# A decoder layer on one core: the hand-written timetable of its engines with many of its places changed

## What is computed

```python
# x, ctx: (4, 512, 512) f32; 16 heads of 32; I = 2048
kqv = x @ Wqkv + bqkv                       # q, k, v
scores = einsum('bsnh,btnh->bnst', k, q) / sqrt(32)
scores = triu(scores) + -10000 * tril(ones, k=-1)
out = einsum('bnkq,bknh->bqnh', softmax(scores, axis=2), v) @ Wo + bo
x = layernorm(x + out)
x = layernorm(x + wkv(w, u, k=x, v=ctx))    # a recurrence over the 512 tokens, per channel
g, up = x @ dequant(gate_w).T, x @ dequant(up_w).T
x = layernorm(x + (silu(g) * up) @ dequant(down_w).T)
```

## Time and profile before

| | us |
|---|---|
| median of 3 runs | 736.33 (734.25 to 738.01) |
| the profiled execution, its own time | 735.65 |
| its span | 733.9 |
| PE busy in the span | 679.5 (93%) |
| DVE, ACT, POOL busy | 548.9, 458.4, 380.2 |

### The profile page before, as it was taken

How to read it: one execution, slowest core, us unless ns; L and a number is a source line. 1 busy time by engine, 2 the same in 40 slices (tenths; PEclk the granted TensorE clock), 3 DMA queues, 4 the chain that set the end, 5 groups by cost and what they waited for, 6 DMA issues and landing times. The chain is left out here.

```text
span 733.9 us, 12511 instructions
## 1 busy us (share of the span) xinstructions
PE 679.5 (93%) x4290; PEld 382.2 (52%) x4290; DVE 548.9 (75%) x1268; ACT 458.4 (62%) x1096; POOL 380.2 (52%) x491
## 2 busy tenths in 40 slices
PE   8889869899996999889899999989999899999997
PEld 3335434445453455445454454534454698568855
DVE  4586735878999898899866598986898778466644
ACT  5698848978798469887764742355552565346620
POOL 6035633753989924774486645485584333303321
PEclk9998989999999999999999999998999999999999
DMA  7868653342315134453053010000000000010001
GB/s 242 248 203 218 164 127 96 117 127 69 116 51 152 35 82 131 116 118 63 2 94 87 1 58 15 29 15 0 1 1 33 25 2 1 1 57 2 1 15 44
DMA packets 45024, 54.33 MB, mean 74 GB/s; under 512 B 5921, under 2 KB 33825, under 8 KB 44961
## 3 DMA queue, kind: packets, MB, share of 16 engines
q1 hardware_dynamic: 41264, 46.85, 21.0%
q0 software_dynamic: 3264, 6.29, 5.2%
q10 hardware_dynamic: 432, 0.39, 0.2%
HBM read 45.00 MB, written 12.71 MB: 79 GB/s over the span
## 5 line engine op out<-in xcount | busy, mean ns | idle before, releaser
L1495 DVE CUSTOM_DVE_ANT_0 ee<-psb,mask,clip 128x512 f32<-128x512 f32 (+3 forms) x256 | 131.0, 537 | 30.4 <-PE psb L1025 29.0
L1263 ACT ACTIVATE ee<-ee,nm 128x512 f32<-128x512 f32 (+3 forms) x256 | 142.2, 559 | 1.9 <-DVE nm L1495 1.9
L1901 POOL TENSOR_TENSOR hl<-ring,hh 128x512 f16<-128x512 f32 x64 | 78.9, 1244 | 97.9 <-ACT hh L1382 62.9
L1273 ACT ACTIVATE ee<-psb 128x512 f32<-128x512 f32 (+1 forms) x192 | 95.6, 522 | 38.2 <-PE psb L1042 24.8
L1832 POOL TENSOR_SCALAR_AFFINE_SELECT ee<-ee 128x256 f32<-128x256 f32 x128 | 55.2, 439 | 76.2 <-ACT ee L1273 75.8
L1170 PE MATMUL psb<-wd,hl 128*128 128x512 f16 x240 | 91.0, 379 | 0.2 <-POOL hl L1901 0.2
L1168 PE MATMUL psb<-wd,hh 128*128 128x512 f16 x240 | 91.0, 379 | 0.0
L1025 PE MATMUL psb<-ks,qs 128*128 128x512 f16 (+3 forms) x256 | 74.4, 308 | 14.2 <-DMA ks<-parts 9.7
L1042 PE MATMUL psb<-qs,ks 128*128 128x256 f16 (+3 forms) x256 | 62.2, 308 | 9.4 <-ACT ee L1273 8.0
L1599 DVE RECIPROCAL ek<-ek 128x128 f32<-128x128 f32 x64 | 58.1, 932 | 6.8 <-POOL ek L1869 6.8
L982 PE MATMUL psb<-xh,wqk 128*128 128x512 f16 x240 | 60.5, 379 | 0.7 <-ACT wqk L1240 0.4
(11 more groups left out here) (213 smaller groups left out, 1630.0 us busy)
## 6 DMA issues: line engine op xcount, KB each, us to landing
qs<-parts SPq DMA_DIRECT2D x48, 128.0 KB, 2.7
ks<-parts SPq DMA_DIRECT2D x45, 128.0 KB, 2.9
parts<-qhl SPq DMA_DIRECT2D x16, 256.0 KB, 2.2
parts<-khl SPq DMA_DIRECT2D x16, 256.0 KB, 2.5
x<-in_x SPq DMA_DIRECT2D x4, 1024.0 KB, 6.6
ct<-in_ctxT SPq DMA_DIRECT2D x4, 1024.0 KB, 5.0
out<-x SPq DMA_DIRECT2D x16, 256.0 KB, 2.0
xt<-in_xT SPq DMA_DIRECT2D x14, 256.0 KB, 3.1
```

What stands on the lines that cost most here:

```text
L1263: e.activation(dst, dst, ACT.Exp, bias=NM[:, n % 4, col:col + 1], scale=-1.0, accum_out=DEN[:, n % 4, col:col + 1]).then_inc(sem("exp"), 1)
L1273: e.activation(ET[H % ET_SLOTS][:, base:base + width], PSB[:, bank["turn", H, item], 0:width], ACT.Exp, scale=SC).then_inc(sem("et"), 1)
L1495: e.tensor_tensor_reduce(E[H % E_SLOTS][:, EOFF[i]:EOFF[i] + w], PSB[:, bank["score", H, i], 0:w], MASK[:, S - w:S], -SC, CLIP[:, i:i + 1] ...
L1901: e.tensor_tensor(HS[it][1][:], pair(b, it // 2)[:, it % 2, :] if b in SEVEN else ring(b, it)[1], HS[it][0][:], ALU.subtract).then_inc(sem ...
```

## The change

Only numbers of the timetable change, and one tuple by which `oh` of groups 0 and 1 is made by ACT instead of POOL. Nothing is added or removed. `WAIT['expand']` is read by nothing. The diff is cut to its core; the rest of the moves, in SV_AT, SPREAD_AT, PV_AT, MQ_AT, MT_AT, WU_ZERO, WG_AT, BO_AT, WO_IN, WD_AT and most of TURN_AT, are of one to five slots:

```diff
-V0_AT = (3, 11)
-QK_AT = {... 3: (17, 26), ... 6: (72, 78), 7: (77, 85), 8: (103, 113), ... 11: (144, 152), ... 15: (216, 222)}
-V_AT = {1: (56, 62, 63, 72), ...}
-WO_AT = {0: (98, 103, 105, 115), ...}
+V0_AT = (0, 11)
+QK_AT = {... 3: (18, 25), ... 6: (73, 80), 7: (78, 86), 8: (103, 117), ... 11: (144, 150), ... 15: (216, 224)}
+V_AT = {1: (54, 61, 63, 74), ...}
+WO_AT = {0: (98, 101, 104, 111), ...}
-EX_AT = {... 4: 94, 5: 109, 6: 125, ... 9: 174, ...}
+EX_AT = {... 4: 86, 5: 106, 6: 121, ... 9: 169, ...}
-WIDE_AT = {... 1: 62, ... 3: 90, ... 5: 123, ... 8: 171, ...}
+WIDE_AT = {... 1: 55, ... 3: 88, ... 5: 122, ... 8: 171, ...}
-STACK_AT = {2: 18, 3: 34, 4: 51, 5: 63, 6: 82, 7: 98, 8: 114, 9: 131, 10: 148, ...}
+STACK_AT = {2: 22, 3: 30, 4: 54, 5: 62, 6: 83, 7: 98, 8: 116, 9: 131, 10: 148, ...}
-WAIT_IN = {'r1': 3, 'norm': 2, 'ek': 0, ...}
+WAIT_IN = {'r1': 0, 'norm': 2, 'ek': 1, ...}
-PIECE_AT = {'load_second': 35, ...}
-WU_AT = (41, 48, 48, 51)
+PIECE_AT = {'load_second': 31, ...}
+WU_AT = (42, 47, 49, 52)
-XLOAD = {1: (2, 2, 20, 26), ..., 3: (125, 140, 147, 162)}
-XSPLIT = {1: (13, 20, 27, 34), ..., 3: (147, 155, 159, 168)}
+XLOAD = {1: (0, 5, 21, 26), ..., 3: (126, 139, 148, 163)}
+XSPLIT = {1: (16, 21, 30, 35), ..., 3: (149, 155, 162, 165)}
-WKV_AT = {..., (3, 0): 1027, (3, 1): 1033, (3, 2): 1035, (3, 3): 1038}
-YT_AT = {..., 1: (1012, 1012, 1013, 1013), 2: (1025, 1028, 1030, 1032), 3: (1044, 1045, 1046, 1050)}
-X2_AT = {..., 2: (1036, 1036, 1036, 1036), ...}
+WKV_AT = {..., (3, 0): 1023, (3, 1): 1033, (3, 2): 1035, (3, 3): 1041}
+YT_AT = {..., 1: (1013, 1013, 1014, 1014), 2: (1026, 1030, 1031, 1032), 3: (1045, 1046, 1047, 1048)}
+X2_AT = {..., 2: (1037, 1037, 1037, 1037), ...}
-ZERO_IN = (3, 5, 5, 7, 8, 8, 9, 9, 9, 10, 11, 11, 12, 12, 12, 14)
-WS_AT = {1: (1020, 1023), 2: (1022, 1027), 3: (1017, 1023), 4: (1031, 1038)}
+ZERO_IN = (5, 7, 7, 10, 10, 10, 11, 11, 11, 12, 12, 13, 14, 14, 15, 17)
+WS_AT = {1: (1020, 1023), 2: (1025, 1027), 3: (1017, 1020), 4: (1032, 1038)}
 TURN_AT: places of turns in groups 0 to 14; of group 2
-  2: ((18, 19, 20), (23, 24, 25), (26, 28, 33), (30, 31, 33))
+  2: ((16, 17, 18), (22, 22, 23), (26, 28, 33), (24, 31, 33))
-OH_POOL = (1, 1, 1, 1, 1, 1, 0, 0, 1, 1, 1, 1, 1, 1, 0, 0)
+OH_POOL = (0, 0, 1, 1, 1, 1, 0, 0, 1, 1, 1, 1, 1, 1, 0, 0)
```

More of the change, by code:

```diff
@@ L69 @@
 W_SPLIT = (9, 14, 15, 19)
-V0_AT = (3, 11)
[L71 to L74, removed]
+V0_AT = (0, 11)
+QK_AT = {2: (12, 19), 3: (18, 25), 4: (37, 44), 5: (44, 50), 6: (73, 80), 7: (78, 86), 8: (103, 117), 9: (124,
+         132), 10: (131, 139), 11: (144, 150), 12: (169, 173), 13: (176, 199), 14: (204, 207), 15: (216, 224)}
@@ L75 @@
+V_AT = {1: (54, 61, 63, 74), 2: (116, 124, 137, 146), 3: (178, 190, 193, 203)}
+WO_AT = {0: (98, 101, 104, 111), 1: (165, 168, 174, 176), 2: (227, 231, 233, 243)}
 EARLY_AT = (246, 276)
-EX_AT = {0: 29, 1: 48, 2: 63, 3: 79, 4: 94, 5: 109, 6: 125, 7: 141, 8: 156, 9: 174, 10: 191, 11: 205, 12: 218,
-         13: 236, 14: 251, 15: 263}
-SV_AT = {0: 34, 1: 52, 2: 66, 3: 82, 4: 98, 5: 114, 6: 130, 7: 146, 8: 162, 9: 177, 10: 196, 11: 210, 12: 226,
+EX_AT = {0: 29, 1: 48, 2: 63, 3: 80, 4: 86, 5: 106, 6: 121, 7: 141, 8: 156, 9: 169, 10: 191, 11: 206, 12: 219,
+         13: 238, 14: 251, 15: 263}
@@ L80 @@
+SV_AT = {0: 34, 1: 53, 2: 66, 3: 83, 4: 98, 5: 114, 6: 130, 7: 150, 8: 162, 9: 177, 10: 198, 11: 210, 12: 226,
          13: 242, 14: 259, 15: 268}
-SPREAD_AT = {0: 34, 1: 50, 2: 66, 3: 82, 4: 98, 5: 113, 6: 128, 7: 146, 8: 161, 9: 176, 10: 194, 11: 210, 12:
-             226, 13: 243, 14: 257, 15: 268}
-PV_AT = {0: 36, 1: 54, 2: 68, 3: 86, 4: 101, 5: 117, 6: 133, 7: 151, 8: 168, 9: 184, 10: 200, 11: 214, 12: 229,
+SPREAD_AT = {0: 32, 1: 50, 2: 65, 3: 82, 4: 98, 5: 114, 6: 128, 7: 146, 8: 160, 9: 176, 10: 194, 11: 210, 12:
+             224, 13: 243, 14: 257, 15: 268}
@@ L84 @@
+PV_AT = {0: 36, 1: 54, 2: 68, 3: 87, 4: 101, 5: 117, 6: 133, 7: 151, 8: 168, 9: 184, 10: 200, 11: 214, 12: 229,
          13: 245, 14: 261, 15: 272}
-WIDE_AT = {0: 43, 1: 62, 2: 77, 3: 90, 4: 103, 5: 123, 6: 139, 7: 152, 8: 171, 9: 185, 10: 203, 11: 219, 12: 235,
-           13: 253, 14: 264, 15: 274}
-MQ_AT = {0: 12, 1: 28, 2: 44, 3: 60, 4: 76, 5: 92, 6: 108, 7: 124, 8: 140, 9: 156, 10: 172, 11: 188, 12: 204, 13:
+WIDE_AT = {0: 43, 1: 55, 2: 78, 3: 88, 4: 103, 5: 122, 6: 139, 7: 152, 8: 171, 9: 185, 10: 203, 11: 218, 12: 237,
+           13: 253, 14: 264, 15: 273}
@@ L88 @@
+MQ_AT = {0: 12, 1: 28, 2: 44, 3: 60, 4: 77, 5: 92, 6: 108, 7: 124, 8: 140, 9: 156, 10: 172, 11: 188, 12: 204, 13:
          220, 14: 236, 15: 252}
-MT_AT = {0: 13, 1: 29, 2: 46, 3: 60, 4: 77, 5: 93, 6: 109, 7: 125, 8: 143, 9: 157, 10: 173, 11: 189, 12: 205, 13:
+MT_AT = {0: 13, 1: 28, 2: 46, 3: 60, 4: 78, 5: 93, 6: 109, 7: 125, 8: 143, 9: 157, 10: 175, 11: 189, 12: 205, 13:
          221, 14: 237, 15: 253}
-STACK_AT = {2: 18, 3: 34, 4: 51, 5: 63, 6: 82, 7: 98, 8: 114, 9: 131, 10: 148, 11: 165, 12: 177, 13: 201, 14:
-            210, 15: 224}
+STACK_AT = {2: 22, 3: 30, 4: 54, 5: 62, 6: 83, 7: 98, 8: 116, 9: 131, 10: 148, 11: 165, 12: 177, 13: 200, 14:
+            210, 15: 220}
@@ L94 @@
 WAIT = {'high': 1, 'low': 1, 'vtake': 2, 'r1': 2, 'norm': 6, 'exp': 4, 'eb': 0, 't1': 1, 't3': 0, 'oh': 2, 'ol':
-        3, 'ek': 1, 'scan_q': 2, 'scan_p': 7, 'divide': 8, 'r2': 2, 'x2h': 0, 'x2l': 0, 'expand': 0}
-WAIT_IN = {'r1': 3, 'norm': 2, 'ek': 0, 'scan_q': 1, 'scan_p': 1, 'divide': 2, 'r2': 0, 'x2h': 0, 'x2l': 0,
+        3, 'ek': 1, 'scan_q': 2, 'scan_p': 7, 'divide': 8, 'r2': 2, 'x2h': 0, 'x2l': 0, 'expand': 4}
+WAIT_IN = {'r1': 0, 'norm': 2, 'ek': 1, 'scan_q': 1, 'scan_p': 1, 'divide': 2, 'r2': 0, 'x2h': 0, 'x2l': 0,
@@ L97 @@
            'norm2': 5}
-PIECE_AT = {'load_second': 35, 'small': 81, 'split_wo': 47, 'load_ds': 180}
-WU_AT = (41, 48, 48, 51)
-WU_ZERO = (56, 124, 127, 150)
-WG_AT = (202, 220, 222, 228)
+PIECE_AT = {'load_second': 31, 'small': 81, 'split_wo': 47, 'load_ds': 180}
+WU_AT = (42, 47, 49, 52)
+WU_ZERO = (55, 119, 126, 149)
+WG_AT = (200, 217, 219, 224)
 WG_ZERO = (221, 228, 242, 243)
-REST_AT = (3, 29, 106, 15)
-BO_AT = (56, 101, 130, 175)
-XLOAD = {1: (2, 2, 20, 26), 2: (62, 65, 82, 92), 3: (125, 140, 147, 162)}
@@ L106 @@
[L106 to L114, removed]
+REST_AT = (1, 29, 106, 15)
@@ new lines @@
+BO_AT = (56, 98, 130, 179)
+XLOAD = {1: (0, 5, 21, 26), 2: (62, 63, 85, 89), 3: (126, 139, 148, 163)}
+XSPLIT = {1: (16, 21, 30, 35), 2: (83, 88, 89, 96), 3: (149, 155, 162, 165)}
+WKV_AT = {(0, 0): 124, (0, 1): 136, (0, 2): 147, (0, 3): 157, (1, 0): 203, (1, 1): 216, (1, 2): 258, (1, 3): 270,
+          (2, 0): 1010, (2, 1): 1015, (2, 2): 1018, (2, 3): 1020, (3, 0): 1023, (3, 1): 1033, (3, 2): 1035, (3,
+          3): 1041}
+YT_AT = {0: (172, 179, 183, 190), 1: (1013, 1013, 1014, 1014), 2: (1026, 1030, 1031, 1032), 3: (1045, 1046, 1047,
+         1048)}
@@ L115 @@
+X2_AT = {0: (224, 225, 228, 233), 1: (1017, 1018, 1018, 1018), 2: (1037, 1037, 1037, 1037), 3: (1056, 1056, 1056,
          1057)}
-WO_IN = (10, 10, 11, 16)
-WD_AT = (258, 258, 259, 263)
-ZERO_IN = (3, 5, 5, 7, 8, 8, 9, 9, 9, 10, 11, 11, 12, 12, 12, 14)
-WS_AT = {1: (1020, 1023), 2: (1022, 1027), 3: (1017, 1023), 4: (1031, 1038)}
+WO_IN = (10, 11, 11, 16)
+WD_AT = (258, 259, 261, 263)
+ZERO_IN = (5, 7, 7, 10, 10, 10, 11, 11, 11, 12, 12, 13, 14, 14, 15, 17)
+WS_AT = {1: (1020, 1023), 2: (1025, 1027), 3: (1017, 1020), 4: (1032, 1038)}
@@ L126 @@
 KEYS = (1, 0, 0, 0)
-TURN_AT = {0: ((20, 21, 25), (22, 25, 26), (27, 29, 32), (31, 31, 32)), 1: ((21, 22, 22), (25, 25, 31), (23, 29,
[9 rows of a table removed]
-OH_POOL = (1, 1, 1, 1, 1, 1, 0, 0, 1, 1, 1, 1, 1, 1, 0, 0)
+TURN_AT = {0: ((20, 21, 25), (23, 26, 27), (27, 29, 32), (30, 31, 31)), 1: ((21, 22, 22), (25, 27, 31), (23, 29,
[9 rows of a table added]
+OH_POOL = (0, 0, 1, 1, 1, 1, 0, 0, 1, 1, 1, 1, 1, 1, 0, 0)
 XH_POOL = (0, 1, 1, 1)
```

## The result

The median of four runs after is 717.54 us (716.1 to 718.85), that of four before 736.17 us: ratio 0.9747, 95% interval 0.9711 to 0.9782, faster by 18.6 us. The profiled execution took 716.1 us, its span is 714.4.

What follows compares the result with a forecast made beforehand. The prediction took the kernel as bound by PE, with holes. Its terms -7.3 - 1.5 - 2.5 - 5.9 - 2 + 4 = -15.2 on 735.65 gave 720.5; with the median 0.7 higher, 721 us, range 711 to 735.

Steps and rivals of the forecast that it cites:

- the likeliest case: Whole kernel: the prediction's own forecast, its summed terms giving 721 us, chance 0.55.
- Slot 60: Group 4's first score: stack lands 3.2 us earlier, work moved ahead 2.5, less half clock 1.6; -7.3 us.
- Start and slots 41 to 48: v units fill slots 0 to 2, first up chunk later, output weight sooner, emx(0) not behind split_x(1, 0); -1.5 us.
- Slots 147 to 170: split_x(3, 0) after group 11's end, stack of group 10 ahead of the load of x; -2.5 us.
- yt(2, 0): Batch 1's yt: placed one gu later, the 2.97 us wait for POOL's y and half clock behind it go; -5.9 us.
- Batch 2's first products: wkv(3, 3) behind the first pair, both waits for ACT's copies go, 4 us put back; -2 us.
- The rest: Turns of all groups, three expands, loads one or two slots later: unseen meetings of five queues cost +4 us.
- rival C: Whole kernel: gains of 5 to 7 us at yt(2, 0) eaten by unseen meetings (+8); 735 us, chance 0.12.
- Rival A: Holes move rather than close: slot 60 gives -2.5, slots 147 to 170 nothing; 728.5 us, chance 0.25.
- the signs of being wrong: PE waits: for L1881 at yt(3, 0), new ones for masks where expands moved, or over 8 us for ACT's L1273.
- Rival B: Batch 2's products: y of wkv(3, 3) late at yt(3, 0), PE stops with all pairs behind; 745 us, chance 0.08.

Runs made afterwards that it cites:

- b_wu_late: Kernel before, with three of four casting loads of the up weight moved behind slot 60 (WU_AT 41, 62, 66, 70): 725.03 us, ratio 0.9860.
- b_early: Kernel before, with the new numbers of everything up to slot 62 and the old ones behind it: 729.52 us, ratio 0.9933.
- b_split11: Kernel before, with only split_x and load_x of batch 3 and qk of group 11 new: 734.86 us, ratio 1.0000.
- a_g9_old: Kernel after, with the old numbers of slots 141 to 176: 718.38 us, ratio to the kernel before 0.9792.
- b_yt2: Kernel before, with only YT_AT[2] new (1026, 1030, 1031, 1032): 732.87 us, ratio 0.9966.
- a_wkv33_old: Kernel after, with wkv(3, 3) and YT_AT[3] of the old table: 719.77 us, ratio to the kernel before 0.9784.
- b_ff: Kernel before, with the new numbers of the feed-forward stage alone: 726.16 us, ratio 0.9908.
- a_relief: Kernel after, with pv(7), x1t of wkv(0, 1) and (0, 2) earlier, reciprocals of wkv(3, 3) and yt(3, ..) later: 716.36 us, ratio to before 0.9732.

## Why the prediction was right, and where it was not

721.0 was forecast, 717.54 measured; the sign, the size and the likeliest case held. That the total came so near is in part luck. By the experiments the terms up to slot 62 are worth 3.9 us less than forecast, those of the feed-forward stage 1.1 less, and everything between 8.4 more, where a loss of 1.5 had been forecast. Term by term:

- **Slot 60, -7.3.** Right in mechanism, and somewhat large. The kernel after wins 6.5 us between slots 44 and 64, the other traces that have all of this part 4.6 to 6.8; the load alone is -3.2 in one direction and 3.3 in the other, and the loads that I took to be the lever are it (b_wu_late). One detail was wrong: the first load went out at 63.32, not some 3 us later, as the mask ahead of it had moved too.
- **Start and slots 41 to 48, -1.5.** Not shown. Everything up to slot 62 is worth -4.9 by the runs, less than slot 60's term alone. In the eight traces with the new start PE stands between 2.0 us ahead and 0.2 behind at slot 44, which is no more than executions differ. A new wait of 2.04 us at slot 27 for ACT's k (4.33 in b_early) was not foreseen: I looked at what v units fill, not at the write of k that ACT must wait for.
- **Slots 147 to 170, -2.5.** The mechanism failed: b_split11, which is that mechanism, gives 0, and in its place PE waits 3.25 us for DVE's shifts. Its rival was in my own text (ACT nearly full), but DVE's shifts behind the recurrence weren't. The stretch as a whole is worth -3.3 (0.1 to 6.5) by a_g9_old, but the traces show 0.1 to 1.6 of it; if the number came out near, it did so for another reason.
- **yt(2, 0), -5.9.** Right at its place (-6.0 just behind it in the kernel after, -5.8 in b_yt2), and wrong as a term that stands alone: without the stage's other moves only 2.5 are kept. The step that failed is the adding of terms as if they were independent; which other move it needs stays open, and wkv(3, 3) isn't it (a_wkv33_old).
- **Batch 2's first products, -2.** Right in the net: PE wins 2.1 us there, and undoing it costs 2.7 by the ratio. Both waits were to go; one of 2.63 us came in their place, within the 4 us that I had put back. With yt(2, 0) it is -6.8 (4.3 to 9.2) by b_ff, against -7.9 forecast.
- **The rest, +4.** Wrong in sign. b_early and b_ff together give 1.59%, or 11.7 us; the whole gives 18.6. The 6.9 us between (about 4 either way, from the three intervals) lie in slots 63 to 250 or in both halves acting together, where I had -2.5 + 4 = +1.5. The traces agree on the sign. From slot 64 to 250 PE wins 3.0 us on the kernel before in the kernel after and 1.1 to 3.6 in the six kernels made from it, but only 0.3 in b_early. That is less than 6.9, and which of the moves does it is open. I had priced unknown meetings at a loss because a loss was the safe side, without a row.

Two numbers of the prediction don't come out of its own terms. With all terms at their bounds the forecast runs from 704 to 748, not from 712 to 728; and rival C's conditions (nothing at yt(2, 0), the rest at +8) give 731, not 735.

Rival A asked for holes that move: one did (slots 147 to 170), slot 60's didn't. Of the signs of being wrong one came, 10.7 us of waits for L1273 instead of 8.0, without the loss that it was to announce. Rival B didn't happen: y of wkv(3, 3) was ready before yt(3, 0), and POOL's last operation for it had landed at 566.5 when PE came at 569.1. Rival C lacked its eight microseconds of new meetings.

## What to carry to other kernels

When a hand-made order is changed, price a hole by its wait and by the work behind it at half clock, and look at what ends it: one that ends on a DMA behind optional transfers closes when these are moved, and one on an engine busy 19.96 of 20 us here only changed its name. Before adding two gains on one engine, follow the earlier arrival to the next places where that engine meets the others: b_yt2 alone kept 2.5 of 5.8 us, and with the rest of its stage new all of it stayed. And moves whose meeting isn't seen have no sign; take them at zero with a wide range, not at a loss.

## What the runs showed of the hardware

**The same program's clock.** Up to slot 240 b_ff runs the same order as the kernel before. In the stretch from 50 to 60 us, before and then b_ff:

```profile
50.00:60.00 10.00, 8.07 (x36) 4.44 (x40) 5.94 (x25) 9.00 (x29) 9.04 (x20) 0.66 0.57 183
```

```profile
50.00:60.00 10.00, 6.33 (x44) 3.21 (x46) 6.91 (x30) 10.00 (x34) 9.55 (x21) 1.00 0.50 140
```

The clock is 0.66 in one and 1.00 in the other, with nothing changed, and PE stands 1.9 us earlier at slot 36. The difference can be larger: b_split11 is 2.4 us behind the kernel before at slot 124, and b_early and the kernel after are 3.9 apart at slot 64, with one order each time. So a difference of 2 us between two single traces of the attention stage says nothing, and one of 4 little; the kernel before ranged from 731.28 to 738.29 in 26 runs.

**DVE beside POOL.** The first L950 in the fence on the products above has both inputs in SBUF and took 2.25 us, and 0.87 later, at 573.01, where POOL was idle. L1558, with one input in PSUM, took 0.68 beside POOL's L1901 at 569.95 and 0.69 without it at 573.80. The scan took 2.34 us beside POOL's products in a_relief and 1.22 alone in the kernel after. The Trainium skill, "SBUF — State Buffer", section "Who interferes with whom", says that a DVE instruction with two SBUF inputs contends with POOL's reads and one with a single such input does not. These durations agree. For the sum it means that a scan's price depends on where it is put.
